# Signs of the ternary weights made by GpSimd instead of ScalarE, and the opening lists in a new order

## The reference, cut to what matters

```python
wg = w.astype(bf16).reshape(-1, 64)                    # groups of 64 weights
scale = clip(mean(abs(wg), -1), 1e-08)
w_ternary = clip(round(wg / scale), -1, 1) * scale     # -scale, 0 or +scale

x = x + tanh(g_xattn) * attention(layernorm(x), ctx)   # projections q, k, v, o, with RMS norms of q and k
h = square(relu(layernorm(x) @ w1.T))                  # w1 = ternary(W_fc): 2048 x 512
x = x + tanh(g_ffn) * (rms_norm(h) @ w2.T)             # w2 = ternary(W_proj): 512 x 2048
```

## Time and profile before

| | |
|---|---|
| time, median of 3 runs | 945.41 us (943.75 to 948.05) |
| span of the profiled execution | 945.4 us |
| PE busy | 894.8 us, 95% |
| ACT busy | 775.4 us, 82% |
| DVE busy | 715.2 us, 76% |
| POOL busy | 572.2 us, 61% |

### The profile page before, as it was taken

One profiled execution on the slowest core, in us unless ns is written; L12 is line 12 of the kernel. 1 busy time (PEld: TensorE's weight loads), 2 busy tenths in 40 slices (PEclk: granted clock), 3 DMA queues, 4 the chain that ended last, 5 costly groups with the idle time before them and its releaser, 6 DMA issues. The chain is left out here.

```text
span 945.4 us, 22870 instructions
## 1 busy us (share of the span) xinstructions
PE 894.8 (95%) x7958; PEld 535.9 (57%) x7958; DVE 715.2 (76%) x1448; ACT 775.4 (82%) x1559; POOL 572.2 (61%) x616
## 2 busy tenths in 40 slices
PE   5677798999999999999999999999999999999998
PEld 2333455466656656656656655556566656556664
DVE  6999999888877778878877778778777778776301
ACT  6888888888888888888888887888888888888673
POOL 1341436657676665657676665757676665757664
PEclk9797999999999999999999999999999999999999
DMA  9558874666666567666667665656765576755300
GB/s 360 141 96 206 201 157 79 113 112 124 120 128 118 110 121 124 123 118 119 120 127 127 100 122 112 122 115 126 121 135 112 105 128 117 127 91 97 68 24 34
DMA packets 319747, 115.80 MB, mean 122 GB/s; under 512 B 305168, under 2 KB 305168, under 8 KB 318096
## 3 DMA queue, kind: packets, MB, share of 16 engines
q1 hardware_dynamic: 319632, 114.34, 61.0%
HBM read 30.67 MB, written 8.39 MB: 41 GB/s over the span
## 5 line engine op out<-in xcount | busy, mean ns | idle before, releaser
L537 PE MATMUL up_pair<-ft,w 128*128 128x256 f16 x960 | 214.5, 273 | 0.2 <-DMA ft<-x_rows 0.2
L538 PE MATMUL up_pair<-ft,w 128*128 128x256 f16 x960 | 214.5, 273 | 0.0
L996 ACT ACTIVATE score_ps<-score_ps,exp_bias,exp_scale 128x128 f32<-128x128 f32 x512 | 189.9, 468 | 4.5 <-DVE exp_bias L1494 4.3
L2025 POOL TENSOR_TENSOR hh_sum<-hh_sum,hh_sb 128x512 f32<-128x512 f32 x112 | 159.1, 1421 | 49.5 <-ACT hh_sb L954 45.2
L552 PE MATMUL mix_ps<-w,big 128*128 128x512 bf16 x448 | 170.0, 380 | 0.7 <-DVE pt L1525 0.7
L553 PE MATMUL mix_ps<-w,big 128*128 128x512 bf16 x448 | 169.8, 379 | 0.0
L2015 POOL TENSOR_TENSOR big<-h_sb,big 128x512 f16<-128x512 f32 x128 | 149.4, 1167 | 25.1 <-POOL big L2015 9.1
L1970 POOL TENSOR_TENSOR ln_rstd<-ln_in,minus_half 128x1 f32<-128x1 f32 x64 | 36.9, 577 | 175.2 <-issue 145.2
L1327 DVE TENSOR_TENSOR p_rows<-score_ps,p_rows 128x512 f16<-128x512 f32 x128 | 85.5, 686 | 50.3 <-ACT p_rows L878 49.5
L878 ACT ACTIVATE p_rows<-score_ps 128x512 f16<-128x512 f32 x128 | 76.0, 639 | 40.1 <-DMA pt<-p_rows 39.8
L927 ACT ACTIVATE h_sb<-up_pair,relu_scale 128x512 f32<-128x512 f32 x120 | 81.7, 681 | 30.1 <-PE up_pair L538 29.8
(11 more groups left out here) (215 smaller groups left out, 2179.1 us busy)
## 6 DMA issues: line engine op xcount, KB each, us to landing
x_sb<-in_x SPq DMA_DIRECT2D x32, 256.0 KB, 3.1
ctx_sb<-in_ctx_t SPq DMA_DIRECT2D x32, 256.0 KB, 4.2
out<-out_sb SPq DMA_DIRECT2D x32, 256.0 KB, 2.3
big<-in_w_fc_t SPq DMA_DIRECT2D x4, 1024.0 KB, 5.3
big<-in_w_proj_t SPq DMA_DIRECT2D x4, 1024.0 KB, 5.9
pt<-p_rows SPq DMA_TRANSPOSE x128, 3.2
big<-in_wq_t SPq DMA_DIRECT2D x1, 1024.0 KB, 4.9
big<-in_wk_t SPq DMA_DIRECT2D x1, 1024.0 KB, 7.1
```

Source lines behind the costliest of these rows:

```text
L537: nc.tensor.matmul(dst[:, half], w, ft[i][:, c, :], start=(c == 0), stop=False)
L538: last = nc.tensor.matmul(dst[:, half], w, ft[i][:, C + c, :], start=False, stop=(c == C - 1))
L996: last = nc.scalar.activation(rows, rows, ACT.Exp, scale=exp_scale[:, :], bias=exp_bias[:, 4 * b + u:4 * b + u + 1])
L2025: nc.gpsimd.tensor_tensor(hh_sum[:, :], hh_sum[:, :], hh_sb[f % 2][:, :], ALU.add).then_inc(hsum_ready, 1)
```

## The change: what it does

- `ternary_sign(p)` moves from ACT to POOL. ACT's Sign (-1, 0, 1) becomes a POOL TENSOR_SCALAR with `is_ge 0.0` and then `subtract 0.5`: plus or minus one half. A weight of zero gets plus one half, and the mask takes it out.
- All ternary weights are thereby half as large. The constant that the relu scale is made from is halved (the relu scale doubles), and `hidden_gain` multiplies by 2.0 in place of 1.0.
- The lists of all five engines up to slot 5 stand in another order. No call is added or dropped but the 16 signs that leave ACT's list and join POOL's. Slots 6 and later are unchanged.

```diff
@@ POOL
+            def ternary_sign(p):
+                s, loads = ternary_stage(p // 2)
+                pool.wait_ge(stage_in[s], 16 * loads)
+                nc.gpsimd.tensor_scalar(ternary_place(p), ternary_source(p), 0.0, 0.5, ALU.is_ge,
+                                        ALU.subtract).then_inc(sign_ready, 1)
...
-                nc.gpsimd.tensor_scalar(h_gain[:, :], h_rms[:, :], out_gain[:, :], 1.0, ALU.mult,
+                nc.gpsimd.tensor_scalar(h_gain[:, :], h_rms[:, :], out_gain[:, :], 2.0, ALU.mult,
...
+            q_norm(0)
             k_weight(0)
-            q_norm(0)
             k_rms_of(0)
             x_norm(1, 1)
+            ternary_sign(0)
+            ternary_sign(1)
+            ternary_sign(2)
             x_norm(2, 2)
+            ternary_sign(3)
             rows_plus_constant(0, 0)
             k_weight(1)
             k_rms_of(1)
             q_norm(1)
+            ternary_sign(4)
+            ternary_sign(5)
+            ternary_sign(6)
+            ternary_sign(7)
             x_norm(3, 3)
...
             x1_norm(0, 0)
+            ternary_sign(8)
+            ternary_sign(9)
...
             x1_norm(1, 1)
+            ternary_sign(10)
+            k_rms_of(3)
             k_weight(3)
...
+            ternary_sign(11)
             x_norm(5, 1)
+            ternary_sign(12)
+            ternary_sign(13)
             hidden_lo(0, 2, 0)
...
+            ternary_sign(14)
...
+            ternary_sign(15)
@@ DVE
-                chain(nc.vector.tensor_scalar(tmp_c[:, 1:2], fc_top_all[:, :], TERNARY_CLIP, D * X_SCALE / R_MAX, ALU.max, ALU.mult))
+                chain(nc.vector.tensor_scalar(tmp_c[:, 1:2], fc_top_all[:, :], TERNARY_CLIP, D * X_SCALE / (2 * R_MAX), ALU.max, ALU.mult))
@@ SP
-            load_x(1, 1)
...
             load_ternary(0)
...
+            load_x(1, 1)
             load_ternary(1)
@@ ACT
-                nc.scalar.activation(ternary_place(p), ternary_source(p), ACT.Sign).then_inc(sign_ready, 1)
...
-            ternary_sign(1)
-            ternary_sign(2)
             key_squares(1)
-            ternary_sign(3)
-            ternary_sign(4)
@@ PE
             ternary_pair(10)
+            ffn_up(0, 2, 0, up_ps, 1)
+            scores(3)
...
+            ffn_up(0, 2, 1, up_ps, 1)
             warm(4, 3)
             project_out(2)
-            ffn_up(0, 2, 0, up_ps, 1)
```

More of the change, by code:

```diff
@@ L474, in _ @@
             store(0, 0)
+            load_x(8, 0)
             transpose_x(7)
-            load_x(8, 0)
             for t in range(6, NT - 1):
@@ L1181, in _ @@
[L1181 to L1192, removed]
+            k_hi(2)
+            query_squares(2)
+            x_hi(3)
+            ternary_abs(5)
+            ternary_abs(6)
+            q_hi(2)
+            ternary_abs(7)
+            attention_hi(1)
@@ L1735, in _ @@
             weight_scale(3, up_ps)
+            context_top(1, up_ps[:, P:2 * P])
+            q_lo(0)
+            k_lo(0)
             value_bias()
-            q_lo(0)
-            context_top(1, up_ps[:, P:2 * P])
-            v_lo_of(0)
-            k_lo(0)
             output_constants()
             context_scale(1, 1)
+            v_lo_of(0)
+            next_rows(2)
             ternary_clip(0)
+            context_lo(1, 1)
             exp_scale_of()
+            score_tops(0)
+            x_lo(1)
@@ new lines, in _ @@
+            probs_lo(1, 2)
+            probs_lo(1, 3)
+            q_out(2)
+            ternary_final(1)
+            ternary_final(2)
+            ternary_signed(3)
+            ternary_final(3)
+            x_lo(3)
+            attention(1, 0)
+            k_lo(2)
+            attention(1, 1)
+            context_top(3)
+            q_lo(2)
+            ternary_mask(4)
+            attention_lo(1)
+            ternary_clip(5)
+            ternary_signed(4)
+            ternary_signed(5)
+            v_lo_of(2)
@@ L1814, in _ @@
+            context_scale(3, 0)
+            x1_stats(0, 0)
+            score_tops(2)
+            context_lo(3, 1)
+            ternary_clip(6)
+            ternary_final(4)
+            ternary_mask(5)
+            ternary_mask(6)
+            probs_lo(2, 0)
+            ternary_signed(6)
+            normed_lo(0)
+            x1_out(1, 1)
             probs_lo(2, 1)
-            ternary_signed(6)
             fc_top_of()
-            ternary_final(4)
+            x1_stats(1, 1)
+            next_rows(4)
@@ L1856, in _ @@
[L1856 to L1872 removed]
+            ternary_half(22)
@@ new lines, in _ @@
+            x1_out(2, 2)
+            ternary_mask(9)
+            probs_lo(3, 1)
+            ternary_signed(9)
+            k_out(4)
+            ternary_final(9)
+            probs_lo(3, 2)
+            x1_stats(2, 2)
+            ternary_half(23)
+            probs_lo(3, 3)
+            q_out(4)
+            ternary_signed(10)
+            ternary_signed(11)
+            ternary_half(24)
+            ternary_mask(10)
+            k_lo(4)
+            q_lo(4)
+            x_lo(5)
+            attention(3, 0)
@@ L1934, in _ @@
             q_out(6)
+            next_rows(7)
             ffn_out(1, 0, mix_ps)
-            x_lo(7)
             x1_out(4, 0)
```

555 lines of the change are left out of this document (242 added, 313 removed).

## The result

The changed kernel takes 958.49 us (median of 4, 956.85 to 959.47), the kernel before 944.69 us on the same chip (median of 4, 943.75 to 948.05). The ratio is 1.0138, 95% interval 1.0124 to 1.0153: slower by about 13 us, above the end of the range.

The account below looks back on a forecast made before the run. DVE was taken to bound the opening and PE the rest. 945.4 - 1.4 (waits for ACT) + 2.4 (DVE held by signs) + 0.1 = 946.5 us; range 938 to 954.

Parts of the forecast that it names:

- What bounds the kernel: Opening bound by DVE, the rest by PE; whole time is the start of tile 5's scores plus about 776 us.
- the test that I had named: If the time behind the scores of tile 5 changes by over 1 us, the split into two regimes is wrong.
- Part 1: 16 signs leave ACT's list, about 15 us less work before 175 us; fewer DVE waits for ACT gain 1.4 us.
- Part 2: 16 signs on POOL at 1.34 us each, 21.4 us in all; POOL has room, so cost 0, up to 4.
- the 0 for POOL's queue: Signs in POOL's list cost nothing as POOL work, with up to 4 us if the queue holds back a norm.
- The late norm of slot 3: Rival: signs 8 to 10 delay slot 3's norms up to 4 us, time about 950.5 us; chance 0.07.
- Part 3: Signs on POOL lengthen DVE's instructions in the opening: +2.4 us, bounds +10.7 and -7.3.
- the mean rate of 0.11: DVE loses 0.11 us for each us of POOL, from 7.3 us of stalls against 64.31 us in the opening.
- the 0.5 from rows 9: Three exp_bias instructions of DVE lose 1.91 us to 3.78 us of POOL; taken as the worst rate.
- the port rival: DVE held by POOL's signs through shared ports at 0.5 us for each us: 954.7 us; chance 0.22.
- Part 4: New order of the lists up to slot 5 takes no work off DVE; costed at 0, with 0.1 us in the sum.

Follow-up runs that it names:

- e15: Changed kernel with 64-column signs on POOL, each followed by four powers and one multiplication of one element (3.7 us held, little data): 955.31 us, ratio 1.0122.
- e10: Order of before, signs off ACT, 64-column signs on POOL placed near where ACT had made them: 945.11 us, ratio 0.9995 to the kernel before.
- e13: Changed kernel with 64-column signs, each followed by one power of one element (1.2 us held, little data): 946.86 us, ratio 1.0019.
- e4: Changed kernel with signs of 64 columns in place of 1024, the rest of w1 and w2 set to zero once: 946.93 us, ratio 1.0021.
- e6: Changed kernel with each sign made a multiplication by 1.0 and by 1.0 of the same 1024 columns: 951.72 us, ratio 1.0064.
- e11: As e10, order of before, but with real signs of 1024 columns on POOL: 951.73 us, ratio 1.0061 to the kernel before.
- e9: Changed kernel with x1_norm(1) and slot 3's key and query norms ahead of signs 8 to 10, load_ternary(6) behind three transposes: 960.71 us, ratio 1.0165.

## Why the prediction was wrong

**What bounds the kernel: right in the main.** The lateness arises in the opening. By the test that I had named, the time behind the scores of tile 5, the change is 0.1 us (776.3 and 776.4), and it passes by luck: 1.6 us are added between tiles 5 and 6 and 1.7 given back later. In e15 the time behind the scores of tile 5 is 779.4 us, 3 more. The opening reaches a tile further than I put it; behind tile 6 all profiles lie within 747.1 to 749.9 us.
The base has a small fault too. I took the span of 945.4 us for the time of its execution. Every profile made since has a time 1.8 to 2.3 us above its span, so that execution took some 947 us (an estimate from these), and was slower than the median. It moves the sum by nothing, but the lateness read against this profile may be some 2 us too small.

**Part 1, the signs leave ACT: the work right, the gain not shown.** ACT's busy time falls as computed; e10 shows a gain of 0.05% with an interval on both sides of none, which reaches past my 1.4 us (0.15%) too.

**Part 2, the same signs on POOL: the step that failed.** Two terms of it fell together, the price of a sign and, by that, the 0 for POOL's queue. I priced the sign at 1.34 us from instructions with other pairs of operations and bounded it by 1.08 and 1.53; it takes 3.72. The bounds were bounds on the size, not on the kind of operation: no row of the trace before showed a comparison or a subtraction of this width. The Trainium skill (GPSIMD Engine Reference, "Elementwise — side-by-side cycle accounting"), which I quoted for it, gives a short body 1.03 cycles an element; the copy and the mult and add pairs are near it (1.04 us for 1024), the sign is at over four times that, and the measurement decides.
The second term of the part, "as POOL work of their own they cost nothing", holds at 1.2 us a sign (e13) and not at 3.7 (e15: +1.22%, against +0.19% for e13). The late norm of slot 3, the rival that I gave 0.07 and 4 us, is what the trace shows at tile 3. I had named its place (signs 8 to 10 ahead of the norms of slot 3), and sized it for signs a third as long.

**Part 3, DVE held by POOL: right in kind, its share in the end small.** DVE's busy time to the scores of tile 5 grew by 4.9 us for 56.5 us more of POOL, 0.09 for each us, near the mean rate of 0.11 that I took; 1.5 of these 4.9 us are in e4 already, with hardly any sign data. With 1.34 us a sign that was +2.4. But the rate isn't one number. In e6 10 us more of POOL than in e4 cost 5.8 us of DVE, 0.6 for each us, above the 0.5 from rows 9; in the old order 45 us more (e11 against e10) cost 1.6. So the port rival (954.7) is refuted for the change; its rate, not its time, is seen in e6 (951.72).
The Trainium skill's rule (SBUF — State Buffer, "SBUF: two separate sides") says that the first to start gets the pair for the whole instruction. The changed kernel's trace doesn't agree: q_rows at 141.08 us takes 1.52 us where its like takes 0.74, and ends at 142.60, while the sign beside it runs from 140.57 to 144.64, and no DVE instruction ahead of 200 us is more than 1.1 us longer than the shortest of its like, beside signs of 3.6 us and more. Nor did rows 8 agree as well as I wrote: k_rows, held until 30.88 and then 0.75 us long, would end at 31.63, and it ended at 31.42.
What these 4.9 us add to the queue's cost is left between nothing and about 0.4%: e15 without data is at 1.0122 and the change at 1.0138, and the intervals overlap. It would be little if DVE's longer instructions stand ahead of a norm for which it waits anyway; that is argued, not shown.

**Part 4, the order at 0: nearly right, with cheap signs.** It costs 1.8 us (e4 against e10, 946.93 and 945.11). With long signs it costs 6.8 (the change against e11). The order puts signs where the norms are due, and more of them in a run: four back to back take 14.78 us of POOL from 53.50 us on. It also puts PE's feed-forward piece ahead of the scores of tile 3. I had counted it as moved into idle time; in the change it holds these scores back by 3.5 us. Which of the two makes the order dear with long signs wasn't tried.

**The sum, made again.** Order with cheap signs 0.2%, POOL's queue at the true length 1.0% (1.0122 less 1.0019), and 0.2% left for the ports, by the intervals anything from none to 0.4%: 1.4%. Left open are why the queue's cost sets in so sharply between 3.3 and 4.1 us a sign, which loads and lists of slots 0 and 3 make that step, what the lower clock adds, and how much the ports do in the change.

## What to carry over

Price an instruction of GpSimd by its pair of operations, not by its opcode and size, and time it alone before it is moved there: the factor between two pairs was 3.6 here. An engine's idle share says nothing about what its in-order list can bear; look for the norm, or the mask, behind the new instructions on which another engine waits, and put a long instruction neither ahead of it nor ahead of its own load. A late wait can move on when the list is mended, as in e9: look for the next one on which another engine waits. Relief of an engine that isn't the bound was worth nothing that could be told (e10) and cannot pay for either.

## What the runs showed of the hardware

- GpSimd, 128x1024, f32 to bf16: mult-mult, add-mult, mult-add and copy 1.04 us at best, one operation alone 2.78 us, the other pairs tried 3.62 to 4.07. A second, idle multiplication made a multiplication 2.7 times as fast (2.78 to 1.04 us).
- The 1.04 us forms vary most in proportion (1.04 to 1.49 us) and lengthened DVE's instructions most: 5.8 us of DVE for 10 us of GpSimd more than in e4, against 3.4 for 50 with the 3.7 us form. The faster form disturbed more for each us in these two kernels; in the old order the long form cost DVE 1.6 us for 45 (e11 against e10).
- No DVE instruction of the changed kernel's first 200 us was lengthened by more than 1.1 us, though the signs beside them take 3.6 us and more.
- 64 columns of the sign take 0.43 us, 1024 take 3.63: 3.3 ns for each further column.
